# Block factors on GpSimd, one shared reciprocal, and two residual additions moved, in a fused linear attention and FP4 feed-forward kernel

## The reference, cut to what matters

```python
xn = layernorm(x)                                  # x: 8 x 2048 x 256, fp32
# attention branch: q, k, v = xn @ W_qkv.T, 16 heads of 16
q = softmax(q) / 4;  k = exp(k)
# buckets of 64 tokens; each sees the sums over the buckets before it
attn = einsum(q, context) * 1 / max(einsum(q, k_cumsum), 1e-6)
a = attn @ W_out.T
# feed-forward branch: every operand is quantized in blocks of 16
def fp4_quant_dequant(x):
    scale = max(max(abs(block)) / 6, 1e-12)        # one per block of 16
    q = nearest of (0, .5, 1, 1.5, 2, 3, 4, 6) to abs(block / scale)
    return sign * q * scale
h = silu(fp4(xn) @ fp4(w_gate).T) * (fp4(xn) @ fp4(w_up).T)   # 704 wide
y = fp4(h) @ fp4(w_down).T
out = x + a + y
```

## Time and profile before

| | |
|---|---|
| median of 3 runs | 1443.69 us (1442.86 to 1446.13) |
| the profiled execution | 1443.55 us, of which the span is 1441.8 us |
| TensorE busy | 1342.2 us, 93% of the span |
| VectorE busy | 1342.9 us, 93% |
| ScalarE busy | 1081.1 us, 75% |
| GpSimd busy | 179.9 us, 12%, 540 instructions |
| DMA | mean 69 GB/s |

### The profile page before, as it was taken

One profiled execution on the slowest core, in us unless ns is written; L12 is line 12 of the kernel. 1 busy time (PEld: TensorE's weight loads), 2 busy tenths in 40 slices (PEclk: granted clock), 3 DMA queues, 4 the chain that ended last, 5 costly groups with the idle time before them and its releaser, 6 DMA issues.

```text
span 1441.8 us, 42471 instructions
## 1 busy us (share of the span) xinstructions
PE 1342.2 (93%) x10702; PEld 955.3 (66%) x10702; DVE 1342.9 (93%) x4030; ACT 1081.1 (75%) x3480; POOL 179.9 (12%) x540
## 2 busy tenths in 40 slices
PE   0149999999999999999999999999999999999997
PEld 0126777777777777777777777777777777777775
DVE  5649999999999999999999999999999999999996
ACT  1588777777777777777777777777777777777772
POOL 1521111110101010101010101010111111110100
PEclk9959999999999999999999999999999999999999
DMA  5002333233334333333333333333332333233324
GB/s 118 0 8 45 65 74 80 56 84 70 76 64 84 70 73 67 84 70 69 70 84 70 68 71 82 70 67 75 77 77 61 78 73 81 56 83 70 76 48 81
DMA packets 293240, 100.00 MB, mean 69 GB/s; under 512 B 258272, under 2 KB 292704, under 8 KB 293216
## 3 DMA queue, kind: packets, MB, share of 16 engines
q1 hardware_dynamic: 293216, 99.73, 33.0%
HBM read 19.99 MB, written 16.78 MB: 25 GB/s over the span
## 4 chain that ended last, share of the span: by engine, by line
PE 91%; ACT 3%; DVE 2%; issue 1%; ACTq 0%; DVEq 0%
PE outp L1163 11%; PE nump L1096 6%; PE unit1a L1032 5%; PE unit0a L1032 5%; PE outp L1165 5%; PE unit1a L1034 5%; PE unit1a L1036 5%; PE unit0a L1034 4%; PE unit0a L1036 4%; PE ctxp L1106 4%; PE unit1b L1034 4%; PE unit1b L1032 4%; PE unit1b L1036 4%; PE unit0b L1036 4%; PE unit0b L1032 4%; PE unit0b L1034 4%
## 5 line engine op out<-in xcount | busy, mean ns | idle before, releaser
L1163 PE MATMUL outp<-w_down_cat,q_rows 128*128 128x256 f16 x1408 | 245.7, 274 | 0.0
L593 ACT ACTIVATE snap<-ctxp,mask 64x68 f32<-64x68 f32 x1024 | 235.2, 307 | 3.2
L548 ACT ACTIVATE att_t<-trp 128x256 f16<-128x256 f32 x256 | 98.1, 383 | 111.0 <-PE trp L1118 106.5
L396 POOL TENSOR_TENSOR var_scaled<-squares,var_mul 128x1 f32<-128x1 f32 x128 | 34.4, 269 | 1134.0 <-ACT scratch L486 1126.3
L1163 PEld LDWEIGHTS outp<-w_down_cat,q_rows 128*128 128x128 f16 x1408 | 138.2, 98 | 16.3
L1165 PE MATMUL outp<-w_down_lo,q_rows 128*128 128x256 f16 x640 | 147.3, 273 | 0.0
L511 ACT ACTIVATE xnt<-trp 128x256 f16<-128x256 f32 x256 | 97.0, 379 | 58.6 <-PE trp L1058 58.6
L774 DVE TENSOR_REDUCE blk<-h 128x44 f32<-128x704 f32 x128 | 123.8, 968 | 0.1
L556 ACT ACTIVATE th<-unit1a,c_g 128x352 f32<-128x352 f32 x128 | 70.9, 554 | 58.8 <-PE unit1b L1036 58.7
L827 DVE TENSOR_TENSOR hx_v<-h,blk 128x704 f32<-128x704 f32 x128 | 111.5, 871 | 0.0
L556 ACT ACTIVATE th<-unit0a,c_g 128x352 f32<-128x352 f32 x128 | 70.8, 553 | 54.0 <-PE unit0b L1036 54.0
(11 more groups left out here) (210 smaller groups left out, 4322.5 us busy)
## 6 DMA issues: line engine op xcount, KB each, us to landing
xring<-x SPq DMA_DIRECT2D x128, 128.0 KB, 2.7
out<-xring SPq DMA_DIRECT2D x128, 128.0 KB, 2.5
xqt<-xq_s SPq DMA_TRANSPOSE x128, 2.4
q_rows<-q_rows SPq DMA_TRANSPOSE x128, 3.5
raw_qkv<-wqkv_t SPq DMA_DIRECT2D x1, 768.0 KB, 7.6
raw_gate<-wgate SPq DMA_DIRECT2D x8, 88.0 KB
raw_up<-wup SPq DMA_DIRECT2D x8, 88.0 KB
raw_down<-wdown SPq DMA_DIRECT2D x1, 704.0 KB, 6.1
```

The lines of the kernel that those rows point to most:

```text
L548: nc.scalar.activation(att_t[:, par, part, :], tr32, ACT.Copy).then_inc(att_split, 1)
L593: nc.scalar.activation(kept[:, :, cols], sums[:, :, cols], ACT.Copy, scale=mask[rows, f, h:h + 1])\
L1163: nc.tensor.matmul(downp, hqt[:, par, m, :], w_down_cat[:, m, :], start=(m == 0), stop=False)
```

## The change

- `block_scales` leaves VectorE. GpSimd's new `block_factors` computes the same factors of h and of x with one `tensor_scalar` each, at the head of its step, before `rstd_of`.
- The row's factor is no longer the maximum over the 44 factors: `row_max` takes the maximum over the blocks' maxima and puts it into a new first column of `blk`, so that the same `tensor_scalar` (45 columns) and the same reciprocal (61 columns) treat it too. `row_scale` and `over_row` go. The factor 2^-23 moves into the constant `c_d` and into a new GpSimd `tensor_tensor` of one column (`over_hrow`), which follows VectorE's reciprocal and which `scales_h` on ScalarE and L896 now read.
- VectorE's step is reordered: `block_max_h` before `block_max_x`, `row_max`, `max_q`, the first addition of `add_up(k-3)`, `shift_q`, its second addition, then the reciprocal (`over_factors`, which waits for GpSimd) and the quantization, whose three rounding steps now follow each other directly.
- ScalarE's `scales_x` waits for GpSimd's factor of x, `factor_of_row` for that of h, `scales_h` for `over_hrow`.
- GpSimd's prologue has one more memset and waits for `h_floor` before the main steps.

```diff
@@ -136,8 +137,8 @@
         drec = sb("drec", [P, 2 * HG, HH])
         att = sb("att", [P, 2, D])
         att_t = sb("att_t", [P, 2, 2, D], fp16)
-        blk = sb("blk", [P, 3, FB + XB])
-        hblk, xblk = blk[:, :, 0:FB], blk[:, :, FB:FB + XB]
+        blk = sb("blk", [P, 3, 1 + FB + XB])
+        hblk, xblk = blk[:, :, 1:1 + FB], blk[:, :, 1 + FB:1 + FB + XB]
         xs_hi = sb("xs_hi", [P, 2 * XB], bf16)
         xs_lo = sb("xs_lo", [P, 2 * XB], fp16)
         xq_s = sb("xq_s", [P, 2, 2, D], fp16)
...
@@ -406,8 +412,27 @@
                 nc.gpsimd.tensor_tensor(shift[:, par, :], neg_mean[:, par, :], rstd[:, par, :], ALU.mult)\
                     .then_inc(rstd_step, 1)
+            def block_factors(t, u):
+                do_h, do_x = is_tile(t), is_tile(u)
+                if do_h:
+                    pool.wait_ge(hq_step, after(t, 6, 2))
+                    if begun(t - 1):
+                        pool.wait_ge(c_row_done, after(t - 1))
+                    pool.sem_inc(pool_turn, 1)
+                    nc.gpsimd.tensor_scalar(blk[:, 1, 0:1 + FB], blk[:, 0, 0:1 + FB], SIX_TIE * 2.0 ** 11, h_floor[:, :],
+                                            ALU.mult, ALU.max).then_inc(h_factor, 1)
+                if do_x:
+                    pool.wait_ge(xq_step, after(u, 5, 1))
+                    pool.sem_inc(pool_turn, 1)
+                    nc.gpsimd.tensor_scalar(xblk[:, 1, :], xblk[:, 0, :], SIX_TIE * 2.0 ** 11, XS * TINY * 2.0 ** 11,
+                                            ALU.mult, ALU.max).then_inc(x_factor, 1)
+                if do_h:
+                    pool.wait_ge(over_factor, u + 1)
+                    nc.gpsimd.tensor_tensor(over_hrow[:, :], blk[:, 2, 0:1], two23[:, :], ALU.mult).then_inc(h_factor, 1)
+
             def step(n, d):
                 k, par, odd = 2 * n + d, d, 1 - d
+                block_factors(k - 1, k + 2)
                 rstd_of(k + 4, par)
...
@@ -425,6 +450,7 @@
                                         q_rows[0:WP, n, 0, :].rearrange("p (x b i) -> p x b i", i=2, b=XB),
                                         ALU.subtract).then_inc(mat_lo[n], 1)
             step(-1, 1)
+            pool.wait_ge(factors, 11)
             for n in range(0, 2):
                 for d in range(2):
                     step(n, d)
...
@@ -559,24 +585,24 @@
             def scales_x(t):
                 if not is_tile(t):
                     return
-                act.wait_ge(xq_step, after(t, 6, 2))
+                act.wait_ge(x_factor, after(t))
                 nc.scalar.activation(xs_hi[:, :].rearrange("p (b i) -> p b i", i=2), twice(xblk[:, 1, :]), ACT.Copy)\
                     .then_inc(x_scaled, 1)
             def factor_of_row(t, par):
                 if not is_tile(t):
                     return
-                act.wait_ge(hq_step, after(t, 9, 4))
+                act.wait_ge(h_factor, after(t, 2, 1))
                 if begun(t - 2):
                     act.wait_ge(o_step, after(t - 2, 2))
-                nc.scalar.activation(c_row[:, par, :], hrow[:, 1, :], ACT.Copy, scale=c_d[:, :]).then_inc(c_row_done, 1)
+                nc.scalar.activation(c_row[:, par, :], blk[:, 1, 0:1], ACT.Copy, scale=c_d[:, :]).then_inc(c_row_done, 1)
             def scales_h(t):
                 if not is_tile(t):
                     return
-                act.wait_ge(hq_step, after(t, 9, 5))
+                act.wait_ge(h_factor, after(t, 2, 2))
                 nc.scalar.activation(hs_hi[:, :].rearrange("p (b i) -> p b i", i=2), twice(hblk[:, 1, :]), ACT.Copy,
-                                     scale=hrow[:, 2, :]).then_inc(h_scaled, 1)
+                                     scale=over_hrow[:, :]).then_inc(h_scaled, 1)
             def snapshot(t):
                 if not is_tile(t):
...
@@ -781,48 +807,29 @@
                 nc.vector.tensor_reduce(xblk[:, 0, :], xn[:, par, :].rearrange("p (b j) -> p b j", j=BL), AX.X, ALU.max,
                                         apply_absolute_value=True).then_inc(xq_step, 1)
+            def over_factors(t, u):
+                do_h, do_x = is_tile(t), is_tile(u)
+                if do_h or do_x:
+                    if do_h:
+                        dve.wait_ge(h_factor, after(t, 2, 1))
+                    if do_x:
+                        dve.wait_ge(x_factor, after(u))
+                    both = slice(0 if do_h else 1 + FB, 1 + FB + XB if do_x else 1 + FB)
+                    nc.vector.reciprocal(blk[:, 2, both], blk[:, 1, both]).then_inc(over_factor, 1)
+
             def hx_after(u, nth):
-                return u * 4 + nth
-
-            def block_scales(t, u):
-                if is_tile(u):
-                    dve.wait_ge(xq_step, after(u, 6, 1))
-                    nc.vector.tensor_scalar(xblk[:, 1, :], xblk[:, 0, :], SIX_TIE * 2.0 ** 11, XS * TINY * 2.0 ** 11, ALU.mult, ALU.max)\
-                        .then_inc(xq_step, 1)
-                if is_tile(t):
-                    dve.wait_ge(hq_step, after(t, 9, 1))
-                    nc.vector.tensor_scalar(hblk[:, 1, :], hblk[:, 0, :], SIX_TIE * 2.0 ** 11, h_floor[:, :], ALU.mult, ALU.max)\
-                        .then_inc(hq_step, 1)
-
-            def over_one(t, u):
-                do_h, do_x = is_tile(t), is_tile(u)
-                if do_h:
-                    dve.wait_ge(hq_step, after(t, 9, 2))
-                    nc.vector.tensor_reduce(hrow[:, 0, :], hblk[:, 1, :], AX.X, ALU.max).then_inc(hq_step, 1)
-                if do_h or do_x:
-                    if do_x:
-                        dve.wait_ge(xq_step, after(u, 6, 2))
-                    both = slice(0 if do_h else FB, FB + XB if do_x else FB)
-                    nc.vector.reciprocal(blk[:, 2, both], blk[:, 1, both]).then_inc(hx_step, 1)
-
-            def row_scale(t):
-                if is_tile(t):
-                    dve.wait_ge(hq_step, after(t, 9, 3))
-                    if begun(t - 1):
-                        dve.wait_ge(c_row_done, after(t - 1))
-                    nc.vector.tensor_scalar(hrow[:, 1, :], hrow[:, 0, :], 2.0 ** -23, None, ALU.mult)\
-                        .then_inc(hq_step, 1)
-
-            def over_row(t):
-                if not is_tile(t):
-                    return
-                dve.wait_ge(hq_step, after(t, 9, 4))
-                nc.vector.reciprocal(hrow[:, 2, :], hrow[:, 1, :]).then_inc(hq_step, 1)
+                return u * 3 + nth
+
+            def row_max(t):
+                if not is_tile(t):
+                    return
+                dve.wait_ge(hq_step, after(t, 6, 1))
+                nc.vector.tensor_reduce(blk[:, 0, 0:1], hblk[:, 0, :], AX.X, ALU.max).then_inc(hq_step, 1)
             def over_scales_h(t, par):
                 if not is_tile(t):
                     return
-                dve.wait_ge(hx_step, hx_after(t + 3, 1))
+                dve.wait_ge(over_factor, t + 4)
                 rows = lambda ap: ap.rearrange("p (o b i) -> p o b i", b=FB, i=2)
                 nc.vector.tensor_tensor(rows(hx_v[:, 0:F]), rows(h[:, par, :]), pairs_of(hblk[:, 2, :]), ALU.mult)\
                     .then_inc(hq_step, 1)
...
@@ -917,20 +924,18 @@
             def step(n, d):
                 k, par, odd = 2 * n + d, d, 1 - d
                 scale_x(k + 1, odd)
+                block_max_h(k - 1, odd)
                 block_max_x(k + 2, par)
-                block_max_h(k - 1, odd)
-                block_scales(k - 1, k + 2)
+                row_max(k - 1)
                 max_q(k + 1, odd)
-                over_one(k - 1, k + 2)
-                row_scale(k - 1)
+                add_up(n, d - 3, 0)
                 shift_q(k + 1, odd)
-                over_row(k - 1)
+                add_up(n, d - 3, 1)
+                over_factors(k - 1, k + 2)
                 over_scales_h(k - 1, odd)
                 over_scales_x(k + 2, par)
                 round_hx(k - 1, k + 2, 0)
-                add_up(n, d - 3, 0)
                 round_hx(k - 1, k + 2, 1)
-                add_up(n, d - 3, 1)
                 round_hx(k - 1, k + 2, 2)
                 gate_h(k, 0, par)
                 low_scales(k - 1, k + 2)
...
@@ -982,7 +987,7 @@
             nc.vector.tensor_scalar(c_gu[:, :], pow2[:, 2:3], pow2[:, 3:4], 2.0 ** -44 * UNTIE ** 2, ALU.mult, ALU.mult).then_inc(factors, 1)
             dve.wait_ge(factors, 7)
             nc.vector.tensor_scalar(wscale[:, :], wscale[:, :], 2.0 ** 14, None, ALU.mult).then_inc(factors, 1)
-            nc.vector.tensor_scalar(c_d[:, :], c_gu[:, :], pow2[:, 4:5], 2.0 ** -12 * UNTIE, ALU.mult, ALU.mult).then_inc(factors, 1)
+            nc.vector.tensor_scalar(c_d[:, :], c_gu[:, :], pow2[:, 4:5], 2.0 ** -12 * 2.0 ** -23 * UNTIE, ALU.mult, ALU.mult).then_inc(factors, 1)
             nc.vector.reciprocal(h_floor[:, :], c_gu[:, :]).then_inc(factors, 1)
             dve.wait_ge(factors, 10)
             nc.vector.tensor_scalar(h_floor[:, :], h_floor[:, :], 2.0 * TINY * 2.0 ** 11, None, ALU.mult).then_inc(factors, 1)
...
```

(27 more changed lines are left out.)

19 lines of the change are left out of this document (10 added, 9 removed).

## The result

The changed kernel takes 1450.04 us in the median of 7 runs (1449.47 to 1452.8); the kernel before took 1444.55 us beside it (7 runs, 1442.86 to 1447.07). The ratio is 1.0038, with a 95% interval of 1.0027 to 1.005: slower. The forecast was 1448.3 in a range of 1443.0 to 1457.0. The profiled execution took 1450.04 us with a span of 1448.3, 6.5 us over the span before. The ratio is worked out from all runs with its interval; it can differ from the ratio of the two medians by up to 0.001.

What follows compares the result with a forecast made beforehand. TensorE was taken to bound the steady tile, with no gap. To 1443.55 us came +5.5 prologue, 0 steady tile, -0.9 tail: 1448.2, or 1448.3 as median; own range 1445.5 to 1451, 8 in 10 from 1443.0 to 1457.

Steps and rivals of the forecast that it cites:

- The prologue: Before the main steps: tiles 0 and 1's factors wait behind GpSimd's long weight instructions, delaying ScalarE and TensorE, +5.5 us.
- The small terms: In the prologue: GpSimd's w_out part takes a third of 3.09 us; VectorE's L697, no longer obstructed by L418, gains 0.84.
- rival 3: Prologue: the waits at tiles 0 and 1 are hidden and the tail decides, 1442.8 us; chance 0.12.
- The steady tile: Main loop: VectorE's path, GpSimd's factors and `over_hrow` add nothing to TensorE's tile, 0 us.
- rival 1: Steady tile: `over_hrow` also loses against L834, ends 0.34 us later, TensorE loses 0.23 a tile: +29, 1477 us; chance 0.13.
- VectorE's busy time: Steady tile: falls by about 0.65 us a tile, while VectorE's path does not shorten.
- GpSimd's factors: Steady tile: take 0.25 and 0.2 us, start at about P-0.4, done by P+0.2, wanted by the reciprocal at P+1.45.
- ScalarE's spare time ahead of `th`: Steady tile: `th` could start at P+3.22 against P+3.33 before, leaving 0.11 us to spare.
- VectorE's spare time: Steady tile: stays at about 0.3 us a tile, with L757 starting at P+4.7.
- the cost of `over_hrow`: Steady tile: held until L827 ends, `over_hrow` ends at P+2.92 and ScalarE's spare time covers it, 0 us.
- The tail: Last steps: the second addition comes earlier, the transposed h is next late, and the last projection starts earlier, -0.9 us.

Runs made afterwards that it cites:

- The extra column: Changed kernel plus one unused one-column GpSimd instruction ahead of `over_hrow`: 1481.77 us, ratio 1.0262 to the kernel before.
- its gap removed: Changed kernel with GpSimd's prologue factors put early and two VectorE semaphore waits moved ahead of the reciprocal: 1445.24 us, ratio 1.001 to the kernel before.
- the mended order: Changed kernel with GpSimd's prologue factors of tiles 0 and 1 computed ahead of the long L443 and L448: 1445.34 us, ratio 1.0002 to the kernel before.
- the products of zeros: Changed kernel with added TensorE matmuls of zeros before the main steps and last projections: 1449.25 us, ratio 1.0037 to the kernel before.
- order, waits and products: Changed kernel with early GpSimd prologue factors, two VectorE waits ahead of the reciprocal, and TensorE products of zeros: 1444.3 us, ratio 0.9989 to the kernel before.

## Why the prediction was right

**The prologue, forecast +5.5: right.** ScalarE's first `xn` happened to start at 43.20, 1.20 earlier than before (44.40; the other profiles lie between 43.0 and 44.6), ahead of anything the change touches. Corrected by it, the second `xs_hi` starts at 85.54 (forecast 85.45) and the first main matmul at 107.40 (forecast 107.3): +5.6. The small terms hold too: w_out's part 1.15 us long (forecast 1.03, a third of 3.09), L723 at 2.29 instead of 3.12. Moving the two factors took all but some 0.4 us of the loss away; rival 3, that it would be hidden, is out. The 1.20 us are luck: without them the profiled execution would have taken some 1451.2 us, just above the forecast's own range of 1445.5 to 1451.

**The steady tile, forecast 0: nearly right in the ordinary tile, wrong in the first tile of a sequence.** From P: reciprocal +1.46 (1.45), L834 +2.02 (2.0), `over_hrow`'s end +2.96 (2.92), `hs_hi` +2.99 (2.96). The release 0.05 us after L834 ends is what the earlier trace rows had shown, and rival 1 did not come. The Trainium skill (SBUF — State Buffer, section "A bandwidth-pool intuition that's wrong (but worth ruling out)") gives about 115 ns, from descriptor writes; for this arithmetic instruction the rows have 0.04 to 0.05 us each time. The Trainium skill's rule (SBUF — State Buffer, section "Who interferes with whom") has one holder at a time, for the whole instruction; the two columns of the experiment, each held for one instruction of VectorE, agree with it.

Several sizes in it were off. VectorE's busy time was to fall by 0.65 us a tile. The durations taken out and put in do come to that (L790, L794, L801, L813 and L820 were 0.84 together, `row_max` is 0.19), but the union fell by 0.09: the small ones had run in the shadow of their neighbours, as L820 and L827 in the earlier trace rows, and dependent instructions that now follow each other overlap nothing. GpSimd's factors took 0.47 and 0.28 us, not 0.25 and 0.2, and start at P+0.17, not at P-0.4, since `row_max` stands right ahead of `qmax` (720.38, 0.19 us long); they are ready at P+1.00, and the reciprocal wants them at P+1.46. ScalarE's spare time ahead of `th` was not 0.11 but about 0.07. `th` starts at P+3.33, the old time to the hundredth, since TensorE still releases it, and 0.34 us after `hs_hi`; where it follows `hs_hi` directly, that distance is 0.27. The extra column bears this out: `hs_hi` 0.34 us later makes `th` 0.28 later. And VectorE's spare time, forecast to stay at 0.3 us, went. L783 starts at P+4.93 instead of P+4.7: 0.17 of the 0.23 is the gap before L867, which the two checks make when no addition covers them, the rest longer instructions (L834 0.89, L818 0.53). VectorE's own pace is now about 10.28 us against TensorE's 10.36 in the mean, some 0.1 us to spare.

The step that failed here is the cost of `over_hrow`, taken as 0 from one ordinary tile. At the three tiles where new sequences start TensorE's step is shorter, 10.06 us before, 10.28 after, and `th` had little idle time to give: it started at P+2.98 and could have started 0.27 us behind `hs_hi`, at P+2.86. `hs_hi` went from P+2.59 to P+3.00 and took `th` with it. VectorE's pace alone would give the same 10.28, but with its gap removed the step still took 10.23 to 10.25. These 3 x 0.2 us are the +0.55 of the table; the mended order, which has them too, shows +0.56.

**The tail, forecast -0.9: the order of events right, the sum wrong.** The last projection of h begins 25.27 us after the last `qmax`, before 26.15: -0.88, with the transposed h as the next late, as forecast. But it waits for that with TensorE idle, and then runs at 1.2 GHz (the granted clock is 0.72 in the mean of 1433 to 1445): 3.77 instead of 2.12 us, +1.65. A matmul was costed at its duration before; that the clock could take it was in no step. The kernel before has such a stretch too: 3 us at a granted clock of 0.50 up to 1433, in its second-last projection, and the last chain runs through it (3.10 us from its first product to its last, against 1.84 in its last projection). By an estimate from these rows, without those 1.26 us its last projection would have been ready 24.9 us behind the last `qmax` and would have waited until about 25.1 for the transposed h, as the changed kernel does. Most of the 0.88 us is thus what the low clock cost the kernel before, and not the work that moved. The same term is missing behind the first main matmul: of the +0.99 in the first three steps, 0.80 is the first step at the low clock (9.59 us against 8.79; 8.62 with the products of zeros). The other 0.19 stay at full clock (second step 9.85 against 9.69, with the products too) and are not explained. The clock's 2.4 us are the largest thing that the sum left out, and with the sequence starts they outweigh the lucky 1.2 us at the beginning: 1448.2 - 1.06 + 0.99 + 0.55 + 1.42 = 1450.1, the profiled 1450.04. That the clock has this size is shown by the products of zeros in one profile; that the change itself causes it is not shown: in timed runs the mended order lies 0.9 us above the kernel before, within what the clock varies from run to run. Of the 2.1 us that separate the spans of these two in their profiles, 1.7 are a low stretch in the third main step.

**Left open.** Which executions get a low stretch. Why VectorE's two additions moved alone lose 9 us, while together with the lighter step they lose none, is answered by its pace: 10.47 us from `qmax` to `qmax` against 10.28, on either side of TensorE's 10.36. Which of the removed instructions makes up these 0.19 us no run shows.

## What to carry to other kernels

Work handed to an idle engine joins that engine's whole program order: look at the prologue, where a small instruction may stand behind a large one that nobody was waiting for. An estimate from one ordinary tile does not hold for the few tiles in which the bounding engine has less to do: look at them separately. Removing busy time from an engine does not shorten its path when what is removed had been covering dependences; count start to start, as in the earlier trace rows. And ask of each instruction on the bounding engine at which clock it will run if it starts after a wait: a step that starts 0.9 us earlier can end 0.8 us later.

## What the hardware showed that I had not expected

- A check of two semaphores that are long satisfied costs VectorE 0.17 us in the hardware loop (0.21 us of gap against 0.04); in the unrolled steps the same two instructions follow at 0.04 (123.66 + 0.41, then 124.11).
- A low stretch of the clock can come in the main steps as well: in five of the profiles the third main step is 1.6 to 1.7 us longer than before, in a sixth (order, waits and products) the second by 1.7 and the third by 1.8. The kernel with the mended order has it here, at a granted clock of 0.70, after 4 us in which TensorE was busy for 2.56; the changed kernel had 4 us with 2.24 busy there, and its clock stayed at 1.00:

```profile
124.00:128.00 4.00, 3.64 (x26) 2.25 (x27) 3.42 (x7) 2.97 (x10) 1.63 (x3) 0.70 0.41 99
```

- While GpSimd works on a long product of two inputs, a VectorE instruction of 0.23 us can take 3.00 (L871 above).
- GpSimd's column instruction beside VectorE's two-input instruction takes 0.89 us, where it takes 0.19 alone; its power of one column went from 0.55 to 0.62 us in the mean.
